# Keeping two expert-weight offsets in registers across a loop round, in the expert stage of a decoder layer

## The chip, the cores and the metric

The kernel runs on one core of a Trainium2 chip. The metric is the device time of one execution in microseconds (us), as a median over runs. One execution was also taken by the profiler; every row below comes from that one.

## What is computed

A decoder layer on x of 2 x 1024 tokens with 256 features: layer norm and self-attention with 16 heads, layer norm and cross-attention to a context of 64 tokens, then layer norm and a mixture of experts. All in float32. Only the last part matters here:

```python
shared = silu(xf @ Sg) * (xf @ Su) @ Sd
probs = softmax(xf @ Wr)                      # 16 experts
topk_p, topk_i = top_k(probs, 2)              # two experts for each token
cw = zeros((T, 16)).at[arange(T)[:, None], topk_i].add(topk_p)
for wg, wu, wd, c in experts:                 # F = 128 hidden features each
    acc += (silu(xf @ wg) * (xf @ wu) @ wd) * c[:, None]
```

## The kernel before

Each engine has its own instruction stream; streams meet only in semaphores. The order of work in each stream is written out by hand.

Up to the routed experts, the kernel does attention, cross-attention, the router and the shared expert. Then every token's row is scattered in DRAM (x_slots) to two slots, sorted by expert, so that a tile of 128 slots belongs to one expert. There are at most 32 + 15 = 47 tiles (SLOT_TILES). Which expert owns a tile is known only at run time: VectorE writes owner_i, 47 whole numbers, each the offset of that expert's weights in the on-chip array of all experts' weights (wflat, memory shared with parts).

The tiles go through a pipeline over the engines. For tile j:

- SyncE loads the tile's rows from x_slots into a ring of four (xt, the memory of kT), four tiles ahead.
- TensorE transposes them (tile_transposes, L1097), ScalarE copies the result to SBUF (tile_in, L1425).
- TensorE multiplies by the gate and up weights of the tile's expert (tile_gate_up, L1105, two products of 256 columns), ScalarE takes the silu of one half (L1430), VectorE multiplies by the other (tile_hidden, L2044).
- TensorE transposes that (tile_hidden_transpose, L1114), VectorE copies it (tile_hidden_in, L2049), TensorE multiplies by the down weights (tile_down, L1122), VectorE copies the result (tile_result, L2054), and GpSimd scatters it to DRAM (y_tok, L590).

In TensorE's stream, step j issues in this order: weights and gate/up of tile j + 1, the hidden transpose of tile j, the transposes of tile j + 3, and the down product of tile j - 1. The offset of a tile's weights is a register value, which tile_weights (L1090) reads out of owner_i with a value load. Gate/up of a tile uses it first and down of the same tile two steps later. Within one call of tile_steps the Python dictionary w keeps the register from the one use to the other.

The 47 steps are tile_steps(0, 4), written out; a hardware loop of five rounds of tile_steps(8 * i + 4, 8) (L1149); and tile_steps(44, 3), written out, with one more tile_down. A register value made in one round can't be named in the next, since the loop's body is one piece of code. So `if i - 1 not in w` loads the offset of tile j - 1 a second time, at i = 0 and i = 1 of each call (at i = 1 alone in the first call, which has no down at j = 0), and the last tile_down loads its own again.

From step 38 on, VectorE also adds finished results into the output (weigh, L2059): eight half-pieces, one in each step, each waiting for loads from y_tok that ScalarE issues at steps 35 to 38 (load_results, L1440). What is left of the results is loaded and added after the last tile, and stored.

Of the kernel before, what the change touches and what calls it, by code (L numbers as in the profile page):

```python
# [40 lines left out]
E_ROUTED, F = 16, 128  # L41
FS = 256
WCOLS = KD * F * 2 + D
TOPK = 2

SLOT_TILES = TOPK * T // P + E_ROUTED - 1
# [25 lines left out]
def decoder_layer(nc, x, ctx_in, wq, wk, wv, wo, w_down, w_up_k, w_up_v, xq_w, xq_b, xkv_w, xkv_b,  # L72
                  xproj_w, xproj_b, wr, wg, wu, wd, sg, su, sd, out):
    with ExitStack() as stack:
# [258 lines left out]
        def after(eng, semaphore, count):  # L333

            if not isinstance(count, int) or count > 0:
                eng.wait_ge(semaphore, count)
# [258 lines left out]
        def _(pe):  # L595
# [201 lines left out]
            with pe.If(short == 1):  # L797
# [5 lines left out]
                n = B * H - 1  # L803
# [17 lines left out]
            with pe.If(short == 0):  # L821
                with pe.Fori(0, B) as b:
                    with pe.Fori(0, KD) as half:
                        with pe.Fori(0, HH) as j:
                            n = b * H + half * HH + j
# [259 lines left out]
            destinations()  # L1085

            def tile_weights(j):

                return pe.value_load(owner_i[0:1, ds(j, 1)], min_val=0, max_val=(E_ROUTED - 1) * WCOLS)  # L1090

            def tile_transposes(j, r):

                pe.wait_ge(s_xt[r], 16 * (j // 4 + 1))
                after(pe, s_tT, j - 1)
                for k in range(KD):
                    mm = nc.tensor.transpose(ps[:, r % 2, k * P:(k + 1) * P], xt[r][:, k * P:(k + 1) * P], ident[:])  # L1097
                mm.then_inc(s_tT_ps, 1)

            def tile_gate_up(j, r, w):  # L1100

                pe.wait_ge(s_tT, j + 1)
                after(pe, s_thid, j - 1)
                for k in range(KD):
                    mm = nc.tensor.matmul(ps[:, 2 + r % 2, 0:2 * F], xtT[r][:, k, :],  # L1105
                                          wflat[:, ds(w + k * 2 * F, 2 * F)],
                                          start=(k == 0), stop=(k == KD - 1))
                mm.then_inc(s_tgu, 1)

            def tile_hidden_transpose(j, r):  # L1110

                pe.wait_ge(s_thid, j + 1)
                after(pe, s_hT, j - 1)
                nc.tensor.transpose(ps[:, 4 + r % 2, 0:F], hid_s[r % 2], ident[:]).then_inc(s_hT_ps, 1)  # L1114

            def tile_down(j, r, w):

                pe.wait_ge(s_hT, j + 1)
                after(pe, s_yt, j - 1)
                if isinstance(j, int) and j == 0:  # L1120
                    pe.wait_ge(s_dest, 1)
                nc.tensor.matmul(ps[:, 6 + r % 2, 0:D], hT[r % 2],  # L1122
                                 wflat[:, ds(w + 4 * F, D)], start=True, stop=True)\
                    .then_inc(s_ty_ps, 1)

            def tile_steps(first, n):

                w = {}
                for i in range(n):
                    j, peeled = first + i, isinstance(first, int)  # L1130
                    if not peeled or j + 1 < SLOT_TILES:
                        w[i + 1] = tile_weights(j + 1)
                        tile_gate_up(j + 1, (i + 1) % 4, w[i + 1])
                    tile_hidden_transpose(j, i % 4)
                    if not peeled or j + 3 < SLOT_TILES:
                        tile_transposes(j + 3, (i + 3) % 4)
                    if not peeled or j > 0:
                        if i - 1 not in w:
                            w[i - 1] = tile_weights(j - 1)
                        tile_down(j - 1, (i - 1) % 4, w[i - 1])  # L1140

            pe.wait_ge(s_wres, 48 * E_ROUTED)
            for j in range(3):
                tile_transposes(j, j)
            pe.wait_ge(s_owner, 1)
            tile_gate_up(0, 0, tile_weights(0))
            pe.wait_ge(s_acc, NCHUNK)
            tile_steps(0, 4)
            with pe.Fori(0, (SLOT_TILES - 7) // 8) as i:  # L1149
                tile_steps(8 * i + 4, 8)  # L1150
            tile_steps(SLOT_TILES - 3, 3)
            tile_down(SLOT_TILES - 1, 2, tile_weights(SLOT_TILES - 1))

        @block.scalar
# [961 lines left out]
```

## Time and profile before

| | |
|---|---|
| median of 3 runs | 612.98 us (612.12 to 613.3) |
| the profiled execution: its own time / its span | 613.19 us / 611.4 us |
| TensorE busy (matmul) over the span | 554.1 us, 91% |
| VectorE / ScalarE / GpSimd busy | 374.5 / 399.1 / 212.6 us |
| the stage of the expert tiles | from 493.25 us (first tile transpose) to about 593 us (last down product) |

```text
span 611.4 us, 14232 instructions
## 1 busy us (share of the span) xinstructions
PE 554.1 (91%) x4551; PEld 300.2 (49%) x4552; DVE 374.5 (61%) x1002; ACT 399.1 (65%) x568; POOL 212.6 (35%) x238
## 2 busy tenths in 40 slices
PE   3995999999999999999999899999999769899960
PEld 2442333333333333333336677767655556666640
DVE  5796555565555655555554488787888624444564
ACT  4477999999999999999993555645443723232310
POOL 4000693494049500000003242280275714444450
PEclk9997899999999999999999999999989979999995
DMA  9923333444444444433404730000022234443746
GB/s 258 367 91 67 71 73 71 75 77 77 78 77 78 76 73 74 74 73 71 84 27 131 200 86 3 2 1 2 2 86 87 90 105 129 119 135 123 254 165 206
DMA packets 53595, 60.20 MB, mean 98 GB/s; under 512 B 10769, under 2 KB 44690, under 8 KB 53554
## 3 DMA queue, kind: packets, MB, share of 16 engines
q1 hardware_dynamic: 46546, 46.19, 31.8%
q0 software_dynamic: 3792, 10.36, 4.7%
q10 hardware_dynamic: 3216, 3.15, 1.5%
q8 instruction: 20, 0.33, 0.2%
q14 instruction: 21, 0.17, 0.1%
HBM read 22.17 MB, written 18.61 MB: 67 GB/s over the span
## 4 chain that ended last, share of the span: by engine, by line
PE 75%; DMA 8%; DVE 7%; issue 4%; ACT 4%; POOL 1%; DVEq 0%; ACTq 0%; POOLq 0%; SPq 0%
PE ps L719 21%; PE ps L709 20%; PE ps L1105 8%; DMA x_slots<-val,place_i 6%; PE ps L1122 4%; PE ps L761 2%; PE ps L862 2%; PE ps L930 2%; PE ps L1097 2%; PE ps L728 2%; DVE ftmp L1776 2%; PE ps L637 1%; DMA qT<-y_tok 1%; PE ps L880 1%; PE ps L898 1%
## 5 line engine op out<-in xcount | busy, mean ns | idle before, releaser
L1632 DVE TENSOR_TENSOR ps<-ps,kstack 128x128 f32<-128x128 f32 (+3 forms) x256 | 123.9, 495 | 103.6 <-PE ps L709 103.5
L1253 ACT ACTIVATE pT<-ps 128x1024 f32<-128x1024 f32 x128 | 124.9, 1022 | 6.3 <-PE ps L709 2.6
L709 PE MATMUL ps<-qstack,kstack 96*128 96x512 bf16 x352 | 93.1, 388 | 4.6 <-issue 4.6
L719 PE MATMUL ps<-pT,vcur 128*32 128x256 f32 x1024 | 80.5, 387 | 0.0
L1253 ACT ACTIVATE xn<-ps 128x1024 f32<-128x1024 f32 x64 | 65.6, 1024 | 9.3 <-PE ps L709 8.2
L590 POOL DMA_INDIRECT y_tok<-ftmp,dest_i x47 | 45.1, 959 | 60.2 <-DVE ftmp L2054 59.9
L1253 ACT ACTIVATE xnT<-ps 128x1024 f32<-128x1024 f32 x64 | 65.2, 1019 | 0.2
L1105 PE MATMUL ps<-parts,xnT 128*128 x188 | 53.9, 411 | 6.4 <-issue 3.7
L709 PEld LDWEIGHTS ps<-qstack,kstack 96*128 96x128 bf16 x352 | 29.2, 98 | 54.7 <-issue 15.6
L1430 ACT ACTIVATE oT<-ps 128x128 f32<-128x128 f32 x47 | 13.0, 278 | 63.1 <-PE ps L1105 63.1
L563 POOL TENSOR_TENSOR resid<-resid,projb 128x512 f32<-128x512 f32 x8 | 10.1, 1266 | 122.4 <-DVE xn L1969 121.8
L719 PEld LDWEIGHTS ps<-pT,vcur 128*32 128x32 f32 x1024 | 26.8, 109 | 38.6 <-issue 15.7
L2044 DVE TENSOR_TENSOR oT<-oT,ps 128x128 f32<-128x128 f32 x47 | 13.5, 288 | 52.1 <-ACT oT L1430 51.7
L1105 PEld LDWEIGHTS ps<-parts,xnT 128*128 128x128 f32 x188 | 32.9, 194 | 24.3 <-issue 21.4
L709 PE MATMUL ps<-early 96*128 96x512 bf16 x160 | 41.4, 381 | 0.0
L719 PE MATMUL ps<-xnT,vcur 128*32 128x256 f32 x512 | 40.9, 391 | 0.0
L584 POOL DMA_INDIRECT x_slots<-val,place_i x32 | 31.6, 989 | 25.9 <-DMA x_slots<-val,place_i 12.3
L719 PE MATMUL ps<-xn,vcur 128*32 128x256 f32 x512 | 39.3, 379 | 0.0
L558 POOL TENSOR_SCALAR xn<-resid,mv,rstd 128x256 f32<-128x256 f32 x14 | 17.0, 1222 | 44.1 <-DVE rstd L1762 44.1
L1122 PE MATMUL ps<-parts,oT 128*128 x94 | 29.4, 395 | 1.7 <-DVE oT L2049 0.7
L997 PE MATMUL ps<-qT,wcur 128*128 128x512 f32 x64 | 30.5, 625 | 0.3 <-DVE att_c L1923 0.3
L327 POOL TENSOR_TENSOR ftmp<-qT,att_c 128x512 f32<-128x512 f32 x6 | 7.6, 1274 | 57.8 <-DMA kstack<-parts 48.2
(299 smaller groups left out, 965.1 us busy)
## 6 DMA issues: line engine op xcount, KB each, us to landing
qstack<-parts SPq DMA_DIRECT2D x132, 64.0 KB, 2.3
x_slots<-wcur SPq DMA_DIRECT2D x1, 6016.0 KB, 21.0
kT<-x_slots SPq DMA_DIRECT2D x47, 128.0 KB, 2.2
kstack<-parts SPq DMA_DIRECT2D x132, 32.0 KB, 2.0
early<-parts SPq DMA_DIRECT2D x60, 64.0 KB, 2.3
resid<-in_x_dram SPq DMA_DIRECT2D x4, 512.0 KB, 5.3
parts<-in_L_ffn_Wg_dram SPq DMA_DIRECT2D x16, 128.0 KB, 2.3
parts<-in_L_ffn_Wu_dram SPq DMA_DIRECT2D x16, 128.0 KB, 2.3
```

Of the source, the lines that this page charges most:

```text
L558: nm = nc.gpsimd.tensor_scalar(xn[:, HT * (h % 2) + t, :], resid[:, i, :], mv[:, i, 0:1], rstd[:, i:i + 1], ALU.subtract, ALU.mult)
L584: nc.gpsimd.indirect_dma_start(x_slots, bass.IndirectOffsetOnAxis(ap=place_i[:, r, t:t + 1], axis=0), xe[:, t, :], None).then_inc(s_scatte ...
L590: nc.gpsimd.indirect_dma_start(y_tok, bass.IndirectOffsetOnAxis(ap=dest_i[:, j:j + 1], axis=0), yt[j % 4], None).then_inc(s_yst[j % 4], 16)
L709: nc.tensor.matmul(ps[:, score_bank(g3, kt) + g, :], kstack[g3][:, kt * P:(kt + 1) * P], qstack[g3][:, 1 - first, 512 * g:512 * (g + 1)], ...
L719: mm = nc.tensor.matmul(ps[2 * HD * g:2 * HD * (g + 1), 6 + r, 0:256], vcur[:, r, kt, :], pT_ring[kt % 4][:, 256 * g:256 * (g + 1)], start ...
L997: mm = nc.tensor.matmul(ps[:, 2 * m + a, :], wcur[:, m, (2 * a + k) * F:(2 * a + k + 1) * F], fT[:, k, c * CHUNK:(c + 1) * CHUNK], start=( ...
L1105: mm = nc.tensor.matmul(ps[:, 2 + r % 2, 0:2 * F], xtT[r][:, k, :], wflat[:, ds(w + k * 2 * F, 2 * F)], start=(k == 0), stop=(k == KD - 1))
L1122: nc.tensor.matmul(ps[:, 6 + r % 2, 0:D], hT[r % 2], wflat[:, ds(w + 4 * F, D)], start=True, stop=True)\
L1253: nc.scalar.activation(pT_ring[kt % 4], two_banks(score_bank(g3, kt)).rearrange("p a n -> p (a n)"), ACT.Exp, bias=-SHIFT).then_inc(s_exp, 1)
L1430: nc.scalar.activation(silu_s[j % 2], ps[:, 2 + j % 2, 0:F], ACT.Silu).then_inc(s_tsilu, 1)
L1632: nc.vector.tensor_tensor(blk, blk, within[:, side, 4 * P - n:] if side == 0 else within[:, side, 0:n], ALU.mult)\
L2044: nc.vector.tensor_tensor(hid_s[r % 2], silu_s[r % 2], ps[:, 2 + r % 2, F:2 * F], ALU.mult).then_inc(s_thid, 1)
```

## The change

The last two offsets of a call of tile_steps are kept for the next call. Two registers, carried[0] and carried[1], are allocated ahead of the loop. At the end of each call but the last, carry moves the offsets of the last two tiles loaded in it into them. At i = 0 and i = 1 of the next call, carried_weights(i) takes a snapshot of carried[i] in place of the load. The first call is handed the offset of tile 0 in its dictionary, and the last tile_down takes the offset that the last call returns. Of the value loads, 47 stay, one for each tile, and 14 go: ten in the five rounds, one in the first call, two in the last, and one at the last tile_down. Nothing else is changed on any engine.

```diff
+            carried = [pe.alloc_register(f"carried{r}") for r in range(2)]
+
+            def carry(w, n):
+
+                for r in range(2):
+                    pe.reg_mov(carried[r], w[n - 1 + r])
+
+            def carried_weights(r):
+
+                return pe.snap(carried[r], min_val=0, max_val=(E_ROUTED - 1) * WCOLS)
+
...
-            def tile_steps(first, n):
-
-                w = {}
+            def tile_steps(first, n, w):
+
...
                         if i - 1 not in w:
-                            w[i - 1] = tile_weights(j - 1)
+                            w[i - 1] = carried_weights(i)
                         tile_down(j - 1, (i - 1) % 4, w[i - 1])
+                if not peeled or j + 1 < SLOT_TILES:
+                    carry(w, n)
+                return w
...
-            tile_gate_up(0, 0, tile_weights(0))
+            w_first = tile_weights(0)
+            tile_gate_up(0, 0, w_first)
             pe.wait_ge(s_acc, NCHUNK)
-            tile_steps(0, 4)
+            tile_steps(0, 4, {0: w_first})
             with pe.Fori(0, (SLOT_TILES - 7) // 8) as i:
-                tile_steps(8 * i + 4, 8)
-            tile_steps(SLOT_TILES - 3, 3)
-            tile_down(SLOT_TILES - 1, 2, tile_weights(SLOT_TILES - 1))
+                tile_steps(8 * i + 4, 8, {})
+            w_last = tile_steps(SLOT_TILES - 3, 3, {})
+            tile_down(SLOT_TILES - 1, 2, w_last[2])
```

## Rows read from the trace of the kernel before

**Rows 1.** The page: busy time of TensorE.
```profile
PE 554.1 (91%) x4551; PEld 300.2 (49%) x4552; DVE 374.5 (61%) x1002; ACT 399.1 (65%) x568; POOL 212.6 (35%) x238
```
**Rows 2.** Busy time by stretch, first and fourth round: PE, PEld, DVE, ACT, POOL, clock, DMA.
```profile
504.80:521.30 16.50, 15.08 (x72) 10.76 (x73) 7.40 (x25) 5.20 (x16) 7.67 (x8) 1.00 0.42 129
...
554.20:570.40 16.20, 15.09 (x73) 10.79 (x73) 7.12 (x25) 5.20 (x16) 7.67 (x8) 1.00 0.41 131
```
**Rows 3.** Timeline of TensorE, fourth round's start: start, us, what, idle before.
```profile
554.21 1.12 PE L1105 MATMUL ps<-parts,xnT 128*128 x4 [0.36 <-ACT xnT L1425]
...
556.69 1.13 PE L1105 MATMUL ps<-parts,xnT 128*128 x4 [0.28 <-issue]
...
559.24 1.13 PE L1105 MATMUL ps<-parts,xnT 128*128 x4 [0.30 <-issue]
...
561.02 1.12 PE L1105 MATMUL ps<-parts,xnT 128*128 x4
```
**Rows 4.** The same timeline at the second round's start.
```profile
521.30 1.13 PE L1105 MATMUL ps<-parts,xnT 128*128 x4 [0.50 <-ACT xnT L1425]
...
524.03 1.13 PE L1105 MATMUL ps<-parts,xnT 128*128 x4 [0.47 <-issue]
...
526.81 1.13 PE L1105 MATMUL ps<-parts,xnT 128*128 x4 [0.49 <-issue]
```
**Rows 5.** Line 1090 over the whole span: ns min/median/max.
```profile
L1090 PEldq TENSOR_LOAD <-owner_i x61: 297/307/889, 494.5 to 591.0; - x61
```
**Rows 6.** Sequencer instructions of one ordinary step, 559.24 to 561.02, line by line.
```profile
L1090 PEldq FUSED_REGOPS  x2: 42/96/151, 560.0 to 560.5; - x2
L1090 PEldq TENSOR_LOAD <-owner_i x1: 311/311/311, 560.1 to 560.1; - x1
L1090 PEldq SEQ_ASSERT  x1: 18/18/18, 560.7 to 560.7; - x1
L336 PEldq EVENT_SEMAPHORE  x4: 51/51/51, 559.4 to 560.8; - x4
L1122 PEldq FUSED_REGOPS  x1: 51/51/51, 559.9 to 559.9; - x1
L1105 PEldq FUSED_REGOPS  x2: 42/46/51, 559.3 to 560.9; - x2
L1094 PEldq FUSED_REGOPS  x1: 97/97/97, 559.5 to 559.5; - x1
```
**Rows 7.** Line 1090 from 522.9 to 526.3, second round.
```profile
L1090 PEldq TENSOR_LOAD <-owner_i x3: 306/482/493, 523.0 to 525.7; - x3
```
**Rows 8.** Line 1149, the loop itself.
```profile
L1149 PEldq FUSED_REGOPS  x5: 68/68/73, 503.5 to 569.3; - x5
L1149 PEldq ALU_OP  x5: 32/32/32, 519.8 to 585.1; - x5
...
L1149 PEldq MOVE  x1: 34/34/34, 503.4 to 503.4; - x1
```
**Rows 9.** Timeline of TensorE before the loop, gate/up of tiles 2 and 3.
```profile
499.08 1.12 PE L1105 MATMUL ps<-parts,xnT 128*128 x4 [0.19 <-issue]
...
501.13 1.13 PE L1105 MATMUL ps<-parts,xnT 128*128 x4 [0.16 <-ACT xnT L1425]
```
**Rows 10.** Timeline of TensorE, then of VectorE, after the loop.
```profile
586.79 1.12 PE L1105 MATMUL ps<-parts,xnT 128*128 x4 [0.60 <-ACT xnT L1425]
...
588.84 1.13 PE L1105 MATMUL ps<-parts,xnT 128*128 x4 [0.18 <-issue]
...
590.31 0.29 DVE L2044 TENSOR_TENSOR oT<-oT,ps 128x128 f32<-128x128 f32 x1 [0.40 <-ACT oT L1430]
```
**Rows 11.** ScalarE's issue at 571.87, its time to landing, VectorE's first weighed piece.
```profile
571.87 0.41 ACTq L1440 DMA_DIRECT2D qT<-y_tok  x1
...
qT<-y_tok ACTq DMA_DIRECT2D x1, 512.0 KB, 4.8
...
577.67 0.87 DVE L2059 SCALAR_TENSOR_TENSOR resid<-val,wtop,resid 128x256 f32<-128x256 f32 x2
```
**Rows 12.** Queues from 522 to 585, and landing of a tile's load, median.
```profile
q14 instruction: 3, 0.02, 0.1%
...
kT<-x_slots SPq DMA_DIRECT2D x28, 128.0 KB, 2.2
```

## The prediction

> **What bounds the kernel now.** I read the page first. TensorE is busy 91% of the span [rows 1], but the change touches only the expert tiles near the end, so I went to the table of busy times by stretch, cut at the rounds of the loop. A round of eight tiles takes 16.2 to 16.5 us, the granted clock is full, and TensorE is busy 15.1 us of it [rows 2]; no other engine comes near its length. So 1.1 to 1.4 us of idle TensorE a round has to come from somewhere, and each round has it in the same place. The timeline shows where. An ordinary step, from one gate/up to the next, takes 561.02 - 559.24 = 1.78 us, with no idle time. The two steps ahead of it take 2.48 and 2.55 us, and the idle time before their gate/up is put down to "issue" [rows 3]: TensorE's sequencer had not yet got there, though nothing in other engines was late. These are the steps with a second value load: the down product at i = 0 and i = 1.
>
> Next I looked at the sequencer's own instructions in one ordinary step. There are twelve. Their durations sum to 42 + 151 + 311 + 18 + 4 x 51 + 51 + 2 x 46 + 97 = 966 ns [rows 6]. With 1.78 us for the step, 0.81 us are left for the gaps between them, 0.07 us for each, and for handing on the matmuls in between. The starts in the rows lie one behind the other without a pause, from 559.3 to 560.9. So the sequencer is occupied all through even the ordinary step, and it is just as long as TensorE's array work. Anything added to it shows in full, and that is what the second load does.
>
> **The change part by part.** *The loads that go.* One value load is a register instruction for the address (42 ns), the load itself (311 ns here, median 307 over 61 [rows 5]), a register instruction of 151 ns and an assert of 18 ns [rows 6]. This makes 522 ns, and four gaps of 0.07 us bring it to 0.80 us. The other way to price it is by what a second load does to a step: 2.48 - 1.78 = 0.70 and 2.55 - 1.78 = 0.77 us [rows 3]. These are the length of the path itself, so I lean to them and take 0.75 us. Ten in the rounds: **7.5 us** less. By the lower of the three prices it is 7.0, by the highest 8.0.
>
> In the second round the two steps take 2.73 and 2.78 us [rows 4], 0.45 us more than in the fourth. Two of the three loads there took 482 and 493 ns instead of 307 [rows 7]. Half or more of the long ones must be loads that stay, so I count nothing of this as gain. The longest load of all, 889 ns [rows 5], is one that stays, right behind the loop. If the long ones became ordinary by chance or by the shifted code, about 0.6 + 0.35 us more would be saved. I take 0 and keep 0.9 for the range.
>
> *The snapshots that come in.* A snapshot with bounds might cost the bounds check as well. The loop makes one of its counter with bounds given, and line 1149 has only plain register instructions, no assert [rows 8]. Then a snapshot is a move of 34 ns [rows 8] with a gap of 0.07, so 0.10 us, or next to nothing where it is fused with the register instruction behind it: fused ones do several things in 42 to 68 ns. I take 0.06 us, ten times: **0.6 us** more. The ends are 0 and, with check and assert (151 + 18 ns and two gaps more, 0.31 us), 10 x 0.41 = 4.1 us.
>
> *The moves at the end of a call.* Two moves stand ahead of the loop's own counter instruction. Alone they are 2 x 0.10 = 0.2 us; fused with it, the 32 ns instruction becomes one of perhaps 68 ns [rows 8], 0.04 us. They are in the open, because the sequencer is late at the loop's edge anyway (0.36 us idle before the round's first gate/up [rows 3]). I take 0.1 us, six times (five rounds and the first call): **0.6 us** more, with ends 0.2 and 1.2. Behind these moves stand the branch and the next tile's load, and the next gate/up waits for those.
>
> *The first call.* Its one removed load lies in the step from 499.08 to 501.13, 2.05 us [rows 9]. The array's work is that of an ordinary step, 1.78, and can't shrink, so **0.3 us** less, not the load's 0.75. Ends 0 and 0.7.
>
> *The last call.* The step from 586.79 to 588.84 takes 2.05 us [rows 10]. It has no transposes, so its array work is below 1.78 and removing a load would save 0.3 us or more. But VectorE's next product waited only 0.40 us for ScalarE [rows 10], since a weighed piece keeps it busy before; so at most 0.4 of it arrives at the end. I take **0.3 us**, ends 0 and 0.5. The second load of this call and that of the last tile_down lie beside waits for VectorE's copies: 0.
>
> *What is not moved.* No DMA, no wait and no semaphore count changes. SyncE's tile loads are issued four tiles ahead and land in 2.2 us [rows 12], against 7.1 us of four ordinary steps. What hangs on TensorE's last product (GpSimd's scatter, the last loads, sums and stores) moves up with it whole.
>
> Sum: - 7.5 + 0.6 + 0.6 - 0.3 - 0.3 = - 6.9 us. The profiled execution took 613.19 us itself (span 611.4 and 1.79 around it), which gives 606.3; the median of the runs lies 0.2 below that execution, so I say **606.1 us**, 1.1% faster.
>
> **What becomes late next.** Once the steps are even, VectorE could be. Its first weighed piece, at 577.67, needs a load issued at 571.87 that landed 4.8 us later, at 576.67 [rows 11]: 1.0 us of slack. Two of the steps between get 0.7 us shorter each, 1.4 us in all, so VectorE would stand waiting some 0.4 us, in order, with the next tile's product behind it. That product is used by TensorE only behind the following gate/up, four matmuls whose record lasts 1.1 us [rows 3], so I expect that this slack takes it. It costs at most 0.4 us if it does not, or takes back the saving of the last call. It is within the range.
>
> **Rivals.**
>
> *Hidden anyway: no change.* If the sequencer ran ahead of the array, a load less would move nothing, and the time would be 613.0. Against it stand the 0.70 and 0.77 us, about a whole load, and the idle time called issue [rows 3]; for it, that some slack could be in other instructions. The Trainium skill ("Advanced Engine Details and Errata", Sequencer Loop) says that other engine instructions can be read and queued while a control instruction executes. By that rule loads would hide behind matmuls, and the kernel would stay at 613; the trace disagrees, with TensorE idle 0.28 to 0.30 us behind each second load. 3%.
>
> *The snapshot keeps its check.* Then 3.5 us more than in my sum: 609.6 us. Against it, the loop's own snapshot without assert [rows 8]. 7%.
>
> *Slower: the loop must be fetched again.* The change alters where the loop's code starts and how long it is. If its body then no longer stayed in TensorE's instruction memory as a whole, each of the four taken back edges would wait for a transfer. The nearest priced one is 128 KB in 2.2 us [rows 12]. Four of these are 8.8 us, more than the 6.9 gained: 613.0 + 1.9 = 614.9 us. It decides from 1.7 us an edge. Against it: the body gets shorter, and from 522 to 585 us only three small packets went over instruction queues, on a stretch with three back edges [rows 12]. The Trainium skill ("Runtime: NRT & Kernel Launch", Instruction fetch mechanics) says that a taken branch to code outside the current two blocks forces a fetch before execution goes on; in this trace no back edge in that stretch shows one. 3%.
>
> *The long loads go too.* 606.1 - 0.9 = 605.2 us. 10%.
>
> **How the numbers follow.** My own sum has 77%, the others 10, 7, 3 and 3. The forecast's own ends: all low prices, 7.0 - 1.0 - 1.2 + 0 + 0 = 4.8 us less (snapshots at 0.10 each), so 608.2; all high prices, 8.0 - 0 - 0.2 + 0.7 + 0.5 + 0.9 = 9.9 less, so 603.1. Both ends need every term at once; I take 604.2 to 609.0, which holds the fourth rival, all but the far corners of the sum, and part of the way to the checked snapshot. A change of 0.2% (1.2 us) is about what a measurement of this kernel can tell from none. Faster by more than that: 0.94 (the sum, long loads, checked snapshot). Same 0.03. Slower 0.03.
>
> **What would show it.** In the changed trace: 47 register loads of owner_i and not 61; the second and third gate/up of each round 1.8 us behind the one before, without idle time called issue; a round of 14.8 to 15.0 us instead of 16.2; small register instructions, without an assert, where the loads were; the first gate/up of a round up to 0.1 us later against the last than now; VectorE idle before the first weighed piece for some 0.4 us, named as a DMA. Wrong would be: rounds of 16 us (hidden), asserts beside the snapshots, packets on the instruction queue in every round, or ordinary steps longer than 1.78 us.

## The result, and the profile of the changed kernel

| | before | after |
|---|---|---|
| median of the runs, us | 613.14 (612.12 to 615.48, 4 runs) | 607.79 (604.97 to 610.6, 4 runs) |
| profiled execution: own time, span, us | 613.19, 611.4 | 608.24, 606.5 |
| ratio after to before, with its 95% interval | | 0.9886 (0.9846 to 0.9926) |

By the ratio the change is faster by 7.0 us of 613.14 (4.5 to 9.4 by the interval). The two medians of the table, of four runs each, lie 5.35 us apart, a quotient of 0.9913; that is inside the same interval. The forecast of 606.1 against 612.98 is a ratio of 0.9888.

The page of the changed kernel gives TensorE the same share as [rows 1]: the change is too small to be seen there.

```profile
PE 552.5 (91%) x4551; PEld 300.6 (50%) x4552; DVE 372.5 (61%) x1002; ACT 399.1 (66%) x568; POOL 213.1 (35%) x238
```

The table by stretch shows it, for the first and the fourth round (columns as in [rows 2]):

```profile
507.21:522.23 15.02, 14.60 (x73) 10.71 (x73) 7.34 (x26) 5.20 (x16) 7.82 (x9) 1.00 0.46 141
...
552.23:567.15 14.92, 14.54 (x73) 10.71 (x73) 7.03 (x25) 5.20 (x16) 7.70 (x8) 1.00 0.49 142
```

A round is 1.3 to 1.5 us shorter than in [rows 2], and TensorE's idle time in it fell from 1.4 and 1.1 to 0.4 us. The other engines do the same work in it. The timeline of TensorE says where (only the gate/up products, now on line 1116): the start of the tiles, the fourth round's start, and the end of the loop.

```profile
502.00 1.13 PE L1116 MATMUL ps<-parts,xnT 128*128 x4 [0.42 <-ACT xnT L1439]
...
507.21 1.12 PE L1116 MATMUL ps<-parts,xnT 128*128 x4
...
552.23 1.12 PE L1116 MATMUL ps<-parts,xnT 128*128 x4 [0.36 <-issue]
...
554.10 1.13 PE L1116 MATMUL ps<-parts,xnT 128*128 x4
...
555.96 1.13 PE L1116 MATMUL ps<-parts,xnT 128*128 x4
...
557.75 1.13 PE L1116 MATMUL ps<-parts,xnT 128*128 x4
...
582.30 1.13 PE L1116 MATMUL ps<-parts,xnT 128*128 x4 [0.62 <-issue]
...
583.81 1.11 PE L1116 MATMUL ps<-parts,xnT 128*128 x4
```

The two steps of 2.48 and 2.55 us in [rows 3] are now 1.87 and 1.86, and the idle time called issue behind them is gone. The ordinary step is as before (1.79 here). The 0.36 us at the round's first gate/up stayed.

The sequencer's own instructions over the whole span: the value load (line 1101), the snapshots (1097), the two moves at the end of a call (1093) and the loop (1163).

```profile
L1101 PEldq TENSOR_LOAD <-owner_i x47: 297/306/917, 498.4 to 582.9; - x47
...
L1101 PEldq SEQ_ASSERT  x47: 18/18/18, 499.0 to 583.5; - x47
...
L1097 PEldq MOVE  x12: 29/29/38, 507.8 to 584.1; - x12
...
L1093 PEldq FUSED_REGOPS  x6: 43/47/52, 505.8 to 580.6; - x6
...
L1163 PEldq FUSED_REGOPS  x5: 68/68/73, 506.1 to 566.1; - x5
L1163 PEldq COMPARE_BRANCH  x5: 79/218/233, 520.9 to 580.7; - x5
```

There are 47 loads where [rows 5] has 61, and as many asserts as loads. A snapshot is one move of 29 ns with no assert. The loop's ALU_OP of 32 ns [rows 8] is gone: it and the two moves are one instruction of 47 ns. The longest load, 917 ns, stands where the one of 889 stood, right behind the loop.

**The sum, part by part.** Each row is worked out from starts of gate/up products, before and after; tile 2's is the 499.08 of [rows 9] and the 502.00 above.

| stretch | before, us | after, us | difference | forecast |
|---|---|---|---|---|
| start of the span to tile 2 | 499.08 | 502.00 | +2.92 | 0 |
| tiles 2 to 5 | 5.76 | 5.21 | -0.55 | -0.2 |
| five rounds | 81.95 | 75.09 | -6.86 | -6.4 |
| tiles 45 to 46, the last step | 2.05 | 1.51 | -0.54 | -0.3 |
| tile 46 to the end of the span | 22.6 | 22.7 | +0.1 | 0 |
| span | 611.4 | 606.5 | -4.9 | -6.9 |

The forecast's -6.4 is -7.5 for the loads, +0.6 for the snapshots and +0.5 for five carries; its -0.2 has the sixth. So from tile 2 to the end the change gave 7.85 us (7.95 less the last 0.1), some 0.95 more than forecast, and this execution reached tile 2 2.9 us later. The instructions ahead of the tiles are the same in both kernels. The experiments' own profiles show how far that start moves without an edit there: from 498.07 to 504.06 us, and 501.02 in a second profile of the kernel before.

Part of it is TensorE's granted clock. It is a mean of 0.86 from 320 to 345 us in the changed kernel's profile and 1.00 in the other; this is that stretch before, and then after (columns as in [rows 2]):

```profile
320.00:345.00 25.00, 22.90 (x163) 16.34 (x152) 11.46 (x36) 10.46 (x21) 7.18 (x6) 1.00 0.53 148
...
320.00:345.00 25.00, 23.87 (x157) 16.50 (x155) 10.75 (x38) 8.62 (x17) 5.02 (x4) 0.86 0.48 137
```

From 331.8 to 338.6 us the clock was at its lower level (0.50, 1.2 GHz). VectorE's first cast of place_i then came at 446.1 instead of 442.2. One other profile, that of the last experiment but one, has the same fall and 445.9; in the ten others that cast came between 441.4 and 443.8, one of them with a fall half as long. The kernel before in turn had the lower level from 491.1 to 497.9 us, over its first two tiles, which gave back 1 us of the 3.9. With the change profiled again there is no fall near 332 us, so the fall is not the change's doing.

### The profile page after: what moved, and what is told of

The parts are those of the page before. It is cut to its first block, busy times and chain, and to the rows that moved or that the text cites. A ratio compares the mean times of both kernels' runs of the same rounds, so it can differ in the third digit from the quotient of the medians.

```text
span 606.5 us, 14193 instructions
## 1 busy us (share of the span) xinstructions
PE 552.5 (91%) x4551; PEld 300.6 (50%) x4552; DVE 372.5 (61%) x1002; ACT 399.1 (66%) x568; POOL 213.1 (35%) x238
## 4 chain that ended last, share of the span: by engine, by line
PE 79%; DVE 10%; ACT 4%; issue 3%; DMA 1%; POOL 1%; DVEq 1%; another core or an unknown queue 1%; ACTq 0%; POOLq 0%
PE ps L719 21%; PE ps L709 20%; PE ps L1116 8%; PE ps L1133 3%; PE ps L997 3%; PE ps L862 2%; PE ps L761 2%; PE ps L930 2%; PE ps L728 2%; PE ps L1010 2%; PE ps L1108 2%; DVE ftmp L1790 2%; PE ps L637 1%; DVE resid L2073 1%; PE ps L880 1%
## 5 line engine op out<-in xcount | busy, mean ns | idle before, releaser
L1116 PE MATMUL ps<-parts,xnT 128*128 x188 | 52.5, 402 | 3.2 <-issue 2.6
```

## The experiments

The theory: TensorE's sequencer is the bound in the rounds, and each second load adds its whole length to its step. The rivals: what was gained came from somewhere else (the end of a call, the code's place, a fetch), or the sequencer has slack, so that only some of a load counts. The first four kernels ran on one chip beside 17 runs of the kernel before (median 614.92 us), the next four on another (615.14, 9 runs), the last two on a third (615.46, 11 runs).

**The change again.** No edit.

> The changed kernel once more, against the kernel before. The profiled execution of the change began the expert tiles 2.9 us later than the one before (gate/up of tile 2 at 502.00 against 499.08). If that is chance, as TensorE's clock and the scatter ahead of it suggest, a new profile has it elsewhere, while the five rounds repeat at 14.9 to 15.1 us each, and the median comes out 7 to 8 us under before. If the change itself delays what is ahead of it, the start is again near 502 and the median 4 to 5 us under before.

Measured: 608.08 us (6 runs), ratio 0.9877 (0.9835 to 0.9918). From tile 2 to tile 46 it took 81.91 us, against 81.81 in the first profile. The kernel before takes 89.76, and 90.03 in its second profile. This stretch repeats to 0.3 us while whole runs of one kernel spread over 6 us, so it decides in what follows. Gate/up of tile 2 started at 502.90, late again, as the expectation had it for a delay by the change; the median is 6.8 us under that of the kernel before, between the two cases. The profiles further down speak against a delay: of the eight other kernels with the same instructions ahead of the tiles, seven start between 498.07 and 501.04, and one at 504.06.

**One offset carried.** The down product at i = 0 loads again; that at i = 1 keeps the carried one.

```diff
-                for r in range(2):
-                    pe.reg_mov(carried[r], w[n - 1 + r])
+                pe.reg_mov(carried[1], w[n])
...
-                            w[i - 1] = carried_weights(i)
+                            w[i - 1] = carried_weights(i) if i == 1 else tile_weights(j - 1)
```

> Only the offset for i = 1 is carried; at i = 0 the down product loads its offset again, as before (six loads come back, five in the rounds and one after the loop). If each second load costs its own length on the sequencer's path, the second gate/up of each round comes 2.5 us behind the first again, the third stays at 1.87, rounds take 15.6 us, and the whole is 3.3 to 3.6 us slower than with the change. If the two loads share one stall, so that only the removal of both helps, rounds are above 15.9 or stay at 15.0.

Measured: 611.35 us (12 runs), ratio 0.9938 (0.9905 to 0.997), 3.3 us above the change on the same chip. Its timeline at the fourth round's start:

```profile
551.61 1.13 PE L1115 MATMUL ps<-parts,xnT 128*128 x4 [0.39 <-issue]
...
554.15 1.13 PE L1115 MATMUL ps<-parts,xnT 128*128 x4 [0.33 <-issue]
...
556.02 1.12 PE L1115 MATMUL ps<-parts,xnT 128*128 x4
...
557.81 1.13 PE L1115 MATMUL ps<-parts,xnT 128*128 x4
```

The step that loads twice is back at 2.54 us with its idle time, and the next stays at 1.87. Over five rounds that step has a mean of 2.64 us against 1.87 in the change, and a round of 15.82 against 15.02. So each of the two loads has its price where it stands, and the gain does not come from the code's place.

**Every down product loads again.** Nothing is carried, and the down products inside a call load too: 94 loads.

```diff
-                        if i - 1 not in w:
-                            w[i - 1] = carried_weights(i)
-                        tile_down(j - 1, (i - 1) % 4, w[i - 1])
-                if not peeled or j + 1 < SLOT_TILES:
-                    carry(w, n)
+                        tile_down(j - 1, (i - 1) % 4, tile_weights(j - 1))
...
-            tile_down(SLOT_TILES - 1, 2, w_last[2])
+            tile_down(SLOT_TILES - 1, 2, tile_weights(SLOT_TILES - 1))
```

> Every down product loads its offset again, in all steps and not only in the first two of a round; nothing is carried. If the sequencer is the bound in ordinary steps too, every step grows from 1.78 to about 2.5 us, a round to 20.3 to 20.8 us, and the whole is some 32 to 34 us slower than the change. If ordinary steps have slack in the sequencer and only the steps at a round's start have none, ordinary steps stay below 2.1 us and the whole is less than 15 us slower.

Measured: 635.63 us (2 runs), ratio 1.0343 (1.0284 to 1.0401), 27.6 us above the change. Three ordinary steps of its timeline:

```profile
539.84 1.12 PE L1116 MATMUL ps<-parts,xnT 128*128 x4 [0.28 <-issue]
...
542.25 1.13 PE L1116 MATMUL ps<-parts,xnT 128*128 x4 [0.28 <-issue]
...
544.65 1.13 PE L1116 MATMUL ps<-parts,xnT 128*128 x4 [0.28 <-issue]
```

An ordinary step takes 2.40 us, where the change takes 1.75 to 1.85. Rounds 2 to 5 take 20.03 to 20.17, and the first 21.70: most of its second loads take 501 to 550 ns where some 300 is the rule, and no run says why. The expectation was 32 to 34 us more than the change, and it is 27.6. So a second load costs about 0.65 us in an ordinary step, and not the 0.7 to 0.8 at a round's start. The forecast's words that anything added to the ordinary step "shows in full" went a little too far.

**No bounds check on the loads.** The value load becomes a plain register load with a snapshot. Nothing else is left out.

```diff
-                return pe.value_load(owner_i[0:1, ds(j, 1)], min_val=0, max_val=(E_ROUTED - 1) * WCOLS)
+                reg = pe.alloc_register(f"offset{len(loaded)}")
+                loaded.append(reg)
+                pe.reg_load(reg, owner_i[0:1, ds(j, 1)])
+                return pe.snap(reg, min_val=0, max_val=(E_ROUTED - 1) * WCOLS)
```

> The change, and each of the 47 value loads is a bare register load with a snapshot, without the bounds check (a register instruction of 151 ns, an assert of 18 ns and two gaps, about 0.29 us). If the sequencer alone sets ordinary steps, they fall from 1.78 to about 1.50 us. If TensorE's array is just behind it, they fall to the array's own work: four passes of 0.215, three of 0.108 and two of 0.215 us make 1.61 us, so 1.61 to 1.66, rounds of 13.4 to 13.8 us with the loop's edge, and the whole 6 to 7 us faster than the change. If the array already sets them at 1.78, nothing changes but the first steps of a round, less than 1.5 us in all.

Measured: 600.98 us (6 runs), ratio 0.978 (0.9742 to 0.9818), 7.1 us below the change. Three gate/up products of its timeline, 1.72 and 1.70 us apart:

```profile
539.58 1.13 PE L1120 MATMUL ps<-parts,xnT 128*128 x4
...
541.30 1.09 PE L1120 MATMUL ps<-parts,xnT 128*128 x4
...
543.00 1.13 PE L1120 MATMUL ps<-parts,xnT 128*128 x4
```

From tile 2 to tile 46 it takes 76.62 us, 5.3 less than the change again; the rest of the 7.1 lies ahead of tile 2, where starts vary. Its rounds of 13.90 to 14.31 us are longer than the 13.4 to 13.8 expected. Removing 151 + 18 ns and their gaps from a step (0.29 us) gave 0.07 us in the ordinary steps, 1.71 us in the mean of 25 where the change has 1.78. The trace says where most of the difference went. The snapshot that comes in is a move of 37 ns, 0.10 us with its gap, and the loads are longer: a mean of 417 ns in these 25 steps, against 326 in the change. The sequencer's instructions still lie one behind the other, so it still sets the step. Why the loads get longer is not shown. The next kernels look for the array's own limit.

**Two rounds of 20 tiles.** Three back edges fewer, and a loop body two and a half times as long.

```diff
-            with pe.Fori(0, (SLOT_TILES - 7) // 8) as i:
-                tile_steps(8 * i + 4, 8, {})
+            with pe.Fori(0, (SLOT_TILES - 7) // 20) as i:
+                tile_steps(20 * i + 4, 20, {})
```

> The change with two rounds of 20 tiles instead of five of 8: three loop edges fewer (branch, counter, moves), and six of the ten snapshots gone. If an edge costs what its step is longer than an ordinary one (2.25 to 2.27 against 1.78, 0.5 us) and the two steps behind it 0.1 us each, three edges fewer save 3 x 0.7 = 2.1 us from gate/up of tile 2 to that of tile 46: 79.7 us instead of 81.8. If a body of 2.5 times the length has to be fetched again at its back edge, the edge step takes several us and instruction packets appear in the second round.

Measured: 605.13 us (5 runs), ratio 0.9831 (0.9806 to 0.9855). Tile 2 to 46 takes 80.31 us, 1.5 less than the change: 0.5 for each edge taken out, with its two snapshots. This is 0.6 less than the 2.1 expected; two of the late steps take 2.03 and 1.96 us, with loads of 582 and 506 ns in them. The edge step that is left, the one in which the loop jumps back, takes 2.28. From 508 to 580 us two and four packets went over the two instruction queues, 0.03 MB each. So nothing speaks for a fetch at an edge, with the long body neither.

**All 47 steps written out.** No loop, so that addresses are constants.

```diff
-            tile_steps(0, 4, {0: w_first})
-            with pe.Fori(0, (SLOT_TILES - 7) // 8) as i:
-                tile_steps(8 * i + 4, 8, {})
-            w_last = tile_steps(SLOT_TILES - 3, 3, {})
-            tile_down(SLOT_TILES - 1, 2, w_last[2])
+            w_last = tile_steps(0, SLOT_TILES, {0: w_first})
+            tile_down(SLOT_TILES - 1, 2, w_last[SLOT_TILES - 1])
```

> All 47 steps written out, nothing carried, 47 checked loads. No edges, and in ordinary steps no register instruction for a load's address or a wait's count (97 + 42 ns and the gaps, about 0.28 us). If the sequencer sets ordinary steps, they fall to 1.5 to 1.65 us, where the array takes over, as in the two written-out steps of the change (1.52 and 1.62); from tile 2 to tile 46 it takes 70 to 74 us, 8 to 12 us less than the change. If fetching straight code stalls TensorE, single steps of 2.5 us and more appear, and it is no faster than the change.

Measured: 597.35 us (5 runs), ratio 0.9718 (0.9697 to 0.9738), the best kernel here that keeps every bounds check. It beats the kernel before and the change. The table by stretch over eight steps from about the gate/up of tile 5, and two later rows of VectorE's timeline:

```profile
503.21:516.20 12.99, 12.99 (x74) 11.38 (x73) 7.08 (x25) 5.18 (x17) 7.26 (x8) 1.00 0.51 164
```

```profile
552.22 0.29 DVE L2055 TENSOR_TENSOR oT<-oT,ps 128x128 f32<-128x128 f32 x1 [2.27 <-ACT oT L1441]
...
563.83 0.88 DVE L2070 SCALAR_TENSOR_TENSOR resid<-val,wtop,resid 128x256 f32<-128x256 f32 x2 [1.05 <-DMA qT<-y_tok]
```

TensorE is busy 12.99 of 12.99 us, 1.62 us a step. This is the array's own length, and the 1.78 of [rows 3] was the sequencer's: the forecast had taken the two to be equal. The unrolled step keeps the load, the clamp and the assert, but not the address instruction (42 ns) nor the one of 97 ns in [rows 6]. From tile 2 to tile 46 it takes 74.51 us, a little more than the 70 to 74 expected and 7.3 less than the change; 2.5 of that are the five edges at 0.5 each. Further on the steps are no longer even. One takes 2.91 us, where VectorE waits 2.27 us for ScalarE, and one 2.38, where VectorE waits 1.05 us for the load before its first weighed piece.

**Written out, and no bounds check.** The last two edits together.

> Written out, and the loads without the bounds check. If the array sets the unrolled steps already, the check was hidden there and this takes the same time as the unrolled kernel within 0.5 us from tile 2 to tile 46. If the sequencer still sets them, it is up to 44 x 0.29 = 13 us faster, down to the array's 1.61 us a step at most.

Measured: 596.43 us (6 runs), ratio 0.9694 (0.9673 to 0.9715). The interval overlaps that of the one before. Its quiet steps are 1.62 us as well. The check that gave 5.3 us with the loop gives nothing that can be told without it: there the sequencer is ahead of the array. The profiled execution, at 601.81 us the longest of the six, has one wait of VectorE that stands out, and a step of 5.08 us beside it, so that tile 2 to 46 takes 77.79 us here and can't be set against the 74.51. The two steps behind take 2.85 and 2.18 us; TensorE's granted clock is at its lower level (0.50, 1.2 GHz) from 570.4 to 573.8 us.

```profile
567.72 0.88 DVE L2074 SCALAR_TENSOR_TENSOR resid<-val,wtop,resid 128x256 f32<-128x256 f32 x2 [4.02 <-DMA qT<-y_tok]
```

**The kernel before, profiled again.** No edit.

> The kernel before, profiled once more. In the first profiles VectorE was held up for some 2 us at the cast of the chosen experts' numbers near 450 us in all kernels with the change, and not in the one before, though VectorE's instructions are the same. If it is chance, this profile may show it too; if it hangs on the change, it does not. Either way the rounds of the expert tiles repeat at 16.2 to 16.7 us.

Measured: 615.02 us, tile 2 at 501.02, tile 2 to 46 in 90.03, rounds of 16.15 to 16.56 us. VectorE's cast of the experts' numbers is held up here too:

```profile
455.43 0.17 DVE L1822 CAST topf<-vcur 128x16 f32<-128x16 uint32 x1 [1.58 <-issue]
```

So that delay does not hang on the change. The start is 1.9 us later than in the first profile of the same kernel. With the starts of the other kernels told under the first experiment, nothing is left that speaks for the +2.92 of the table being the change's.

**Written out, with more time for the load.** The weighing of a piece comes one step later after its load.

```diff
-        COMB_STEP = LOAD_STEP + 3
+        COMB_STEP = LOAD_STEP + 4
```

> Written out as before, and VectorE's eight weighed pieces start one step later, at step 39 instead of 38. In the unrolled kernel VectorE waited 1.05 us for the load from y_tok ahead of the first piece, and TensorE waited behind it. If that wait is what the last steps lose, it is gone here (one step of 1.62 us is more than 1.05), the steps from 38 on get some 1 us shorter in all, and the last piece, now behind the last tile's products, gives 0.2 to 0.9 us back: 0 to 1 us faster than the unrolled kernel. If the lost time there comes from transfers in each other's way, it stays.

Measured: 602.29 us (6 runs), ratio 0.9779 (0.9741 to 0.9818), against 0.9718 without the edit on another chip. The wait before the first piece is gone and tile 2 to 46 takes 73.46 us instead of 74.51. One step of 2.80 us is left, in which TensorE's transposes wait 0.47 us for a tile's load from x_slots. This execution reached tile 2 at 504.06, with the fall of the clock near 332 us told above. The plain unrolled kernel was not run on this chip, so whether the edit costs anything is not shown.

**Written out, both loads of a piece together.** ScalarE issues both loads of a piece at one step, in the first two steps of the loads.

```diff
-                if LOAD_STEP <= j < LOAD_STEP + TOPK * NFIRST:
-                    load_results((j - LOAD_STEP) % TOPK, (j - LOAD_STEP) // TOPK)
+                if LOAD_STEP <= j < LOAD_STEP + NFIRST:
+                    for r in range(TOPK):
+                        load_results(r, j - LOAD_STEP)
```

> Written out, and ScalarE issues both loads of a piece in one step (35 and 36) instead of one in each of the steps 35 to 38. The second load of the first piece then starts about 1.6 us earlier. If VectorE's wait of 1.05 us hangs on that start, it is gone, at the price of 0.4 us more of ScalarE at steps 35 and 36, which has that much to spare: about 1 us faster than the unrolled kernel. If the loads are bound by the transfers around them, both land later and the wait stays.

Measured: 600.71 us (6 runs), ratio 0.977 (0.973 to 0.981). VectorE no longer waits for a load there, but two steps of 2.27 and 2.93 us remain; VectorE's timeline has this ahead of them:

```profile
567.09 0.42 DVE L2066 COPY ftmp<-ps 128x256 f32<-128x256 f32 x1 [0.88 <-DMA y_tok<-ftmp,dest_i]
```

The row names a buffer that the scatter had not yet let go. Both edits removed the wait that they were made for, and neither gave a lower ratio than the plain unrolled kernel had on its chip.

## Why the prediction was right, step by step

**The bound.** Right for the steps that changed. The kernel with one of the two loads put back is 0.80 us a round longer, 0.77 of it in the one step. The sequencer is the bound in the loop's ordinary steps as well: a load more makes them 0.65 longer, and taking the check away makes them 0.07 shorter. In the change itself, the ordinary steps whose load happens to take 362 to 401 ns are 1.81 to 1.85 us long, the others 1.75 to 1.79. What was wrong is that the array's work was put at the same 1.78 us. It is 1.62, as the unrolled kernel shows. The missing 0.16 us a step was there to be had, and the forecast did not see it.

**The loads that go.** Taken at 0.75 us each. The second and third steps of a round together were 1.26 to 1.37 us shorter in the first, third, fourth and fifth round, 0.66 us net for each step; with the snapshot's 0.09 that is 0.75 for the load, the forecast's price. In the second round it was 1.76, as the loads of 482 and 493 ns [rows 7] are gone there. Ten loads give 7.9 us instead of 7.5. The extra 0.4 is the fourth rival in part; its other part, the longest load behind the loop, did not happen.

**The snapshots.** Taken at 0.06 us and found at 0.09: from the start of the 29 ns move to the next instruction on the sequencer, and from the ordinary 1.78 us to the 1.87 of these steps. So 0.9 us for ten instead of 0.6. The rival that they would keep their check is refuted by the 12 moves without an assert.

**The moves at the end of a call.** Taken at 0.1 us. They were fused with the counter's instruction, 47 ns for 32, and the four edge steps inside the loop (those in which it jumps back) sum to 9.15 us before and 9.18 after. So 0.02 us or less each, and 0.5 us of the sum did not appear.

**The first and last calls.** The first step went from 2.05 to 1.73 us, the 0.3 forecast, but the two behind it also gained, 0.23 together (1.72 to 1.62 and 1.99 to 1.86). The forecast had stopped at the step itself, with the array's 1.78 us as the floor that it can't go under; 1.73 and 1.62 are under it. The last step gave 0.54 us, of which 0.1 was lost behind it: some 0.4 at the end, for the 0.3 forecast and the 0.4 named as its limit. That 0.1 tells little: in the two profiles of the kernel before, the stretch behind tile 46 differs by 0.4 us (22.6 and 22.2).

**VectorE's new wait.** This did not happen in the change. Its first weighed piece, and ScalarE's issue of that load:

```profile
573.11 0.87 DVE L2073 SCALAR_TENSOR_TENSOR resid<-val,wtop,resid 128x256 f32<-128x256 f32 x2
```

```profile
568.64 0.41 ACTq L1454 DMA_DIRECT2D qT<-y_tok  x1
```

From issue to piece it is 4.47 us and VectorE was not idle. The load landed sooner than the 4.8 us of [rows 11], which was one sample. In the two unrolled kernels, with shorter steps, the wait is there (1.05 and 4.02 us). So the mechanism is real, and the change does not reach it.

**The rivals that did not come.** A fetch at every edge: from 536.5 to 583 us, with two taken edges in it, the two instruction queues moved three packets:

```profile
q8 instruction: 1, 0.02, 0.1%
q14 instruction: 2, 0.02, 0.1%
```

Hidden anyway: refuted by the rounds. In the loop, with addresses in registers, a load more costs 0.65 us a step and does not hide behind matmuls. In the unrolled kernel the load hides: 477 ns of load, clamp (the instruction of 151 ns) and assert stand in a step of 1.62 us in which TensorE is never idle. So a load hides where the sequencer's own work for a step is shorter than the array's, and the limit lies between these two kernels. The Trainium skill ("Advanced Engine Details and Errata", Sequencer Loop) says that other engine instructions can be read and queued while a control instruction executes. The unrolled kernel's trace agrees, and the looped kernel's second loads do not.

**In all**, -0.4 (loads), +0.3 (snapshots), -0.5 (carries), -0.4 (first and last calls) and +0.1 (ordinary steps, 1.785 us in the mean and not 1.781, 25 times) make -0.9 us, against the 0.95 by which the stretch from tile 2 on gave more than forecast. That the forecast's 6.9 falls on the 7.0 of the runs is luck: by the trace the change is worth 7.85 (from tile 2 to 46 it is 7.95 by the first two profiles and 8.12 by the second two). The runs' own 7.0 us (4.5 to 9.4) can't tell 6.9 from 7.85; only the trace can.

Two readings of the prediction are off and change nothing in its sum. The second round's two steps are 0.48 us longer than the fourth's, and not 0.45. Fused register instructions take 42 to 151 ns in [rows 6], and not 42 to 68.

**What stays open.** Why the start of the tiles varies by 6 us between profiles of kernels that are alike up to there; the clock's falls, near 332 us and at the first tiles, are a part of it, and the rest has no cause on record. Why the offset of tile 45 takes 889 to 921 ns to load in five kernels with a loop (some 300 is the rule). It need not be the loop: the unrolled kernel without checks has 886 ns for the same tile, while the unrolled kernel's longest load is 578 ns and that of the kernel that loads for every product 601. Why the no-check kernel's loads are longer. What makes ScalarE late for the step of 2.91 us in the unrolled kernel. None of these was tried.

## What to carry to other kernels

Where a matmul loop reads its weights at offsets from registers, add up the durations and gaps of the sequencer's own instructions for one step and set them against the array's work, and not against the step's length: the step is the longer of the two, and a step without idle time need not be the array's. A value load is worth keeping in a register as soon as that sum is the longer one, and writing the loop out, which takes the address work away as well, brought more here than the change itself (ratio 0.9718 against 0.9886). Once the steps get shorter, look at once for loads and buffers that were timed against the old ones.

## What the runs showed of the hardware

- On TensorE's sequencer a checked value load costs 0.65 to 0.77 us where the sequencer is the bound, though the load itself is 306 ns. The clamp (151 ns), the address (42), the assert (18) and the gaps are the rest.
- A snapshot with bounds is a move of 29 ns, and moves ahead of the loop's counter are fused with it at 15 ns more.
- The taken back edge is a compare-and-branch of 218 ns, the last one, not taken, of 79. An edge step is 0.5 us longer than an ordinary one (2.25 to 2.40 against 1.78).
- Matmul records keep their 1.1 us and leave no idle time between steps of 1.78 us, though the array needs only 1.62; with the sequencer ahead the record of the same four matmuls is 1.03 us. A small lateness of issue hides in the records.
- TensorE's granted clock was at its lower level for 6.8 us from 332 us in two of twelve profiles. VectorE's first cast of place_i came at 446 us in these, and at 441.4 to 443.8 in the ten others.
